# A selective scan on one Trainium2 core: in each step ScalarE does the preparation's work before the unit's decay instead of after it

## The chip, the core and the metric

The kernel runs on one core of a Trainium2 chip. The core has five engines that matter here, each with an instruction queue of its own that is worked off in order: TensorE (PE, matmuls into PSUM), VectorE (DVE), ScalarE (ACT), GpSimd (POOL) and SyncE (SP, which issues most DMAs). They meet only at semaphores. The metric is device microseconds from start to end of one execution. All times below are of single executions or medians of them.

## What is computed

The input is x, 8 images of 96 channels and 64x64 pixels. A first layer (a 17x17 depthwise convolution, a pointwise product, gelu, a gate) gives a new x of the same shape. The second layer takes each image as a sequence of 4096 tokens and runs a selective scan over it, forward and backward:

```
xn = layernorm(x) * ln_g + ln_b
x, z = split(xn @ W_in)
x = silu(causal_conv(x, conv_w, conv_b))
proj = x @ W_xproj
dt = softplus(proj[:6] @ W_dt + b_dt)
Bm, Cm = proj[6:22], proj[22:38]
h = exp(dt * A) * h + dt * Bm * x        # along the tokens, 192 channels x 16 states
y = sum over states(h * Cm) + x * D
out = forward((y * silu(z)) @ W_out) + the same backward
```

The change lies in the scan, which is most of the time.

## The kernel before, in words

The scan works on pieces of 1024 tokens (T), 4 pieces of each of 8 images, each piece forward and backward: 64 *rounds* (`LAST = 2 * ITERS`), a loop of 32 iterations with two directions in each. The 192 channels x 16 states of a piece are 3072 rows, cut into 24 *units* (`UNITS`) of 128 rows. For a unit n:

- ScalarE makes the decay exp(dt*A), 128x1024 (L1116), into one of 4 `decay` tiles, or for the five units in `POOL_UNITS = (2, 6, 11, 15, 19)` into a PSUM tile `u_ps`. Right behind it it copies the last column of the scan of unit n-4 to `ends` (L1132), which raises `kept`. Both wait for a scan: the decay of unit n for the scan of n-4 (of n-3 for a unit of the five), the copy for the scan of n-4.
- TensorE spreads B over the rows into one of three `u_ps` tiles (L1029), after the scan of n-3; VectorE multiplies it by dt*x (`drive`, L1204). For the five units GpSimd makes that product instead (`drive_p`, L1246), and TensorE and VectorE have nothing to do for them there.
- VectorE scans along the tokens (L1222) into one of four `hring` tiles. It waits for the decay, the product, the `kept` of unit n-4 and the `c_applied` of unit n-4, that is until GpSimd has read the `hring` tile that is to be written again.
- GpSimd multiplies the scan by C (`hc`, L1259) and raises `c_applied`. TensorE sums over the states into `y_ps` (L1047, two units at a time), ScalarE copies that to `y_sb` every eighth unit (L1180), SyncE stores it.

Beside this runs the *preparation* of the next rounds, a share of it in each of the 24 steps. All its products go through one PSUM bank, `prep_ps`. TensorE writes it, ScalarE copies it out and raises `prep_out`, TensorE writes the next product:

- step 0: ScalarE takes silu of the convolved x (`xa`, L1149), between two loads of its function table;
- step 2: TensorE makes the low-rank product (L1081, L1084), step 3: ScalarE copies it to `low` (L1155);
- steps 4, 6, 8: TensorE makes three parts of dt (L1091, L1091, L1095). Steps 5, 7, 9: ScalarE takes |dt| to `soft` (L1165) and relu to `dt_sb` (L1166); at 7 (parts one and two together) and at 9 it takes exp and then ln of `soft` (L1169, L1171), which raises `soft_step`;
- steps 7 and 9: GpSimd adds `soft` and `dt_sb` (L1266), which is softplus; steps 8 and 10: it multiplies by `xa` (L1270). Step 5: it splits B (L1273, L1275);
- steps 10 to 20: TensorE does the causal convolution of the round after next in three parts, ScalarE copies them to `xc` (L1139) at steps 13, 17 and 21.

The order on each engine is written out by the helper `run`, the same for all: in step m it calls the tasks in the order in which they are named. "front" does the work on the unit that is 8 ahead (`LEAD = 8`): step m makes the decay of unit m+8. "back" does the output of unit m, "prep" and "conv" the preparation. On GpSimd "front" in step m is the `drive_p` of unit m+10, if there is one, and the `hc` of unit m+5; on VectorE it is the drive of unit m+7 and then the scan of unit m+6. Below, "scan 12" is the scan of unit 12 of the round looked at, "step 7" is step 7 of `run`.

Of the kernel before, what the change touches and what calls it, by code (L numbers as in the profile page):

```python
# [96 lines left out]
def load_exp_ln(nc):  # L97

    nc.scalar.add_instruction(mybir.InstLoadActFuncSet(name=nc.get_next_instruction_name(), act_func_set_id=EXP_LN, ins=[], outs=[]))
# [571 lines left out]
def scan(nc, d, w):  # L671

    with ExitStack() as ctx:
# [149 lines left out]
        def run(eng, *tasks):  # L823

            def ahead(kind, pn):
                for m in range(UNITS):
                    for has, what in tasks:
                        if has == kind:
                            what(m, pn, 0, pn)

            ahead("conv", 0)
            ahead("prep", 0)
            for n in range(LEAD):
                for kind, what in tasks:
                    if kind == "front":
                        what(n, n, 0, 0)
            ahead("conv", 1)
            with eng.Fori(0, ITERS) as it:
                for dr in range(2):
                    p = 2 * it + dr  # L840
                    for m in range(UNITS):
                        n = m + LEAD
                        where = (n, it, dr) if n < UNITS else (n - UNITS, it + dr, 1 - dr)
                        for kind, what in tasks:
                            if kind == "front":
                                what(UNITS * p + n, *where)
                            elif kind == "back":
                                what(m, p, it, dr)
                            elif kind == "prep":
                                what(m, p + 1, it + dr, 1 - dr)  # L850
                            else:
                                what(m, p + 2, it + 1, dr)
                    for kind, what in tasks:
                        if kind == "back":
                            what(UNITS, p, it, dr)

        with nc.Block() as block:
# [156 lines left out]
            def _(pe):  # L1014
# [17 lines left out]
                def back(m, p, it, dr):  # L1032

                    if m == UNITS:
                        return
                    g = m // 8
                    if m % 2:
                        n0 = m - 1
                        pe.wait_ge(c_applied, UNITS * p + n0 + 2)
                        if n0 % 8 == 0:  # L1040

                            pe.wait_ge(y_ready, NG * p + g)
                        for n in (n0, n0 + 1):
                            _, q, b = group(n)
                            for i in range(2):
                                at = 32 * (2 * b + i)
                                last = nc.tensor.matmul(y_ps[at:at + 32, :], w["gather"][:, :], hc[n % NHC][:, i * SL:(i + 1) * SL],  # L1047
                                                        start=(q == 0), stop=(q == QN - 1))
                        last.then_inc(summed, 2)
                    if m % 8 == SKIP_AT:  # L1050
                        for b in range(2):
                            for i in range(2):
                                at = 32 * (2 * b + i)
                                if g < 2:
                                    rows, cols, steps = slice(0, P), slice(64 * g + 32 * b, 64 * g + 32 * b + 32), PART[i]
                                else:
                                    rows, cols, steps = slice(64 * i, 64 * i + 64), slice(P + 32 * b, P + 32 * b + 32), PART[2]
                                nc.tensor.matmul(y_ps[at:at + 32, :], w["skip"][rows, cols], xa[dr][rows, steps], start=False, stop=False)
# [42 lines left out]
            def _(act):  # L1101
# [79 lines left out]

                act.wait_ge(zeroed, 1)
                load_exp_ln(nc)
                run(act, ("back", back), ("front", front), ("prep", prep), ("conv", conv))

            @block.vector
            def _(dve):
# [312 lines left out]
```

## Time and profile before

| | us |
|---|---|
| time, median of 3 runs (lowest to highest) | 6072.25 (6064.57 to 6073.67) |
| the profiled execution's own time | 6072.92 |
| its span, first to last instruction | 6071.1 |
| VectorE busy | 5288.1 |
| GpSimd busy | 5088.1 |
| TensorE busy, matmuls | 4711.1 |
| ScalarE busy | 3204.5 |

The span has three stages: the first layer and the normalisation until about 880 us, the scan until about 5800 us, the output projection from there to the end. Busy time is the union of the instructions' times on an engine; the shares are of the whole span. An idle time of an engine is put down to what released it, inferred from semaphores: where an instruction waits for several, it is the one that came last by the profile.

### The profile page before, as it was taken

Reading aid. Unit: us, or ns where it says so; the run is one execution under the profiler, and the core shown is the slowest. Engines: PE = TensorE matmul, PEld = TensorE weight load, DVE = VectorE, ACT = ScalarE, POOL = GpSimd, SP = SyncE. Lnnn points to the kernel's source line nnn. Section 1 sums busy time; section 2 is a strip of 40 time slices with the busy share of each in tenths; the row PEclk is TensorE's granted clock in tenths of the full one; section 3 lists DMA queues with packets and bytes.
Section 4 is the critical chain, followed back from the end, with each engine's and each line's share of the span. In section 5 each row is a group of like instructions: output and inputs, shape, how many; then the busy total and the mean of one; then the engine's idle time right before and its main releaser. Section 6 shows DMA issues by size and latency. Waiting matters only on the chain. (4 is left out here: it accounts for less than half of the span.)

```text
span 6071.1 us, 73617 instructions
## 1 busy us (share of the span) xinstructions
PE 4711.1 (78%) x17230; PEld 1200.4 (20%) x17230; DVE 5288.1 (87%) x3523; ACT 3204.5 (53%) x5159; POOL 5088.1 (84%) x2405
## 2 busy tenths in 40 slices
PE   7998757777777777777777777777777777777788
PEld 6775211111111111111111111111111111111122
DVE  3223749999999999999999999999999999999943
ACT  1224645555555555555555555555555555555533
POOL 0000349999999999999999999999999999999965
PEclk9999876666676666666666666666666666666689
DMA  1002755555555555555555555555555555555599
GB/s 35 28 28 67 213 152 183 184 183 183 184 184 184 184 184 182 182 181 181 182 181 181 182 183 184 184 184 183 182 182 184 184 184 182 183 183 182 182 260 274
DMA packets 351020, 1048.25 MB, mean 173 GB/s; under 512 B 66820, under 2 KB 101430, under 8 KB 300556
## 3 DMA queue, kind: packets, MB, share of 16 engines
q1 hardware_dynamic: 336652, 1022.72, 53.2%
q10 hardware_dynamic: 14336, 25.17, 1.3%
q8 instruction: 12, 0.20, 0.0%
q14 instruction: 20, 0.16, 0.0%
HBM read 836.01 MB, written 211.63 MB: 173 GB/s over the span
## 5 line engine op out<-in xcount | busy, mean ns | idle before, releaser
L1259 POOL TENSOR_TENSOR hc<-hring,c_rep 128x1024 f32<-128x1024 f32 x1541 | 3597.5, 2361 | 18.9 <-DVE hring L1222 13.6
L1222 DVE TENSOR_TENSOR_SCAN hring<-decay,carry,u_ps 128x1024 f32<-128x1024 f32 x1221 | 2827.7, 2333 | 44.3 <-POOL hc L1259 44.3
L1029 PE MATMUL u_ps<-stack_b,w_spread 48*128 48x512 bf16 x2442 | 1053.8, 523 | 908.0 <-DVE hring L1222 904.0
L1116 ACT ACTIVATE decay<-dt_rep,w_a 128x1024 f32<-128x1024 f32 x1222 | 1399.5, 1147 | 675.2 <-DVE hring L1222 662.4
L1204 DVE TENSOR_TENSOR u_ps<-u_ps,u_rep 128x1024 f32<-128x1024 f32 x1221 | 1471.5, 1205 | 68.3 <-DMA u_rep<-u_scr 56.4
L1047 PE MATMUL y_ps<-hc,w_gather 128*32 128x512 f32 x6144 | 1212.4, 874 | 0.0
L1116 ACT ACTIVATE u_ps<-dt_rep,w_a 128x1024 f32<-128x1024 f32 x322 | 360.0, 1118 | 1360.7 <-DVE hring L1222 1360.7
L1246 POOL TENSOR_TENSOR drive_p<-u_rep,b_rep 128x1024 f32<-128x1024 f32 x322 | 760.2, 2361 | 11.1 <-DMA u_rep<-u_scr 11.1
L1222 DVE TENSOR_TENSOR_SCAN hring<-u_ps,carry,drive_p 128x1024 f32<-128x1024 f32 x321 | 751.3, 2341 | 11.6 <-ACT decay L1116 11.6
L666 POOL TENSOR_TENSOR xs<-xc_ln,rs 96x512 f32<-96x512 f32 x64 | 90.3, 1411 | 701.9 <-ACT rs L650 684.2
L1029 PEld LDWEIGHTS u_ps<-stack_b,w_spread 48*128 48x128 bf16 x2442 | 147.4, 101 | 2407.3 <-DVE hring L1222 2004.4
L1068 PE MATMUL prep_ps<-xn,w_conv 128*128 128x512 f32 x792 | 587.6, 848 | 45.4 <-DMA xn<-xn_scr 23.6
L294 PE MATMUL pc<-xpad,toep 128*128 128x256 f32 x1728 | 468.3, 401 | 2.6 <-DVE toep L191 0.6
L191 DVE COPY toep<-pw 128x288 f32<-128x288 f32 x200 | 91.5, 457 | 326.6 <-PE pw L273 326.6
L294 PEld LDWEIGHTS pc<-xpad,toep 128*128 128x128 f32 x1728 | 296.0, 190 | 37.8 <-issue 11.3
L1266 POOL TENSOR_TENSOR dt_sb<-soft,dt_sb 128x1024 f32<-128x1024 f32 (+1 forms) x130 | 237.0, 1823 | 77.3 <-ACT soft L1171 77.3
L1095 PE MATMUL prep_ps<-low,w_dt 6*64 6x512 f32 x260 | 128.1, 1083 | 186.8 <-ACT dt_sb L1166 186.8
L1132 ACT COPY ends<-hring 128x1 f32<-128x1 f32 x1540 | 270.7, 176 | 0.0
L1071 PE MATMUL prep_ps<-xn,w_conv 128*64 128x512 f32 x792 | 254.2, 727 | 1.6 <-ACT xc L1139 1.6
L191 ACT COPY toep<-pw 128x288 f32<-128x288 f32 x200 | 79.9, 399 | 330.1 <-PE pw L273 330.1
L1047 PEld LDWEIGHTS y_ps<-hc,w_gather 128*32 128x32 f32 x6144 | 140.2, 126 | 554.8 <-issue 410.1
L1091 PE MATMUL prep_ps<-low,w_dt 6*128 6x512 f32 x260 | 203.6, 873 | 59.2 <-ACT low L1155 57.8
(108 smaller groups left out, 3966.9 us busy)
## 6 DMA issues: line engine op xcount, KB each, us to landing
dt_rep<-dt_scr SPq DMA_DIRECT2D x194, 1024.0 KB, 5.8
u_rep<-u_scr SPq DMA_DIRECT2D x194, 1024.0 KB, 7.7
c_rep<-bc_scr SPq DMA_DIRECT2D x260, 512.0 KB, 4.0
b_rep<-bc_scr SPq DMA_DIRECT2D x130, 512.0 KB, 4.2
xn<-xn_scr SPq DMA_DIRECT2D x132, 384.0 KB, 5.4
y_scr<-y_sb SPq DMA_DIRECT2D x768, 64.0 KB, 1.6
xn<-xn_scr SPq DMA_DIRECT2D x132, 256.0 KB, 4.7
dt_scr<-dt_sb SPq DMA_DIRECT2D x260, 128.0 KB, 2.1
```

The lines of the kernel that those rows point to most:

```text
L294: last = nc.tensor.matmul(pc[c][:, 0:B * XH].rearrange("p (b x) -> p b x", b=B), toep[par][:, n0:n0 + 2, :].rearrange("p a y -> p (a y)"), ...
L1029: mm = nc.tensor.matmul(u_ps[nv % NSLOT][:, sl], w["spread"][:, q, :], upper(stack_b[drv][:, sl]), start=True, stop=True)
L1047: last = nc.tensor.matmul(y_ps[at:at + 32, :], w["gather"][:, :], hc[n % NHC][:, i * SL:(i + 1) * SL], start=(q == 0), stop=(q == QN - 1))
L1068: mm = nc.tensor.matmul(prep_ps[:, :], w["conv"][:, j, 0:P], xn[:, j, PART[g]], start=(j == 0), stop=(j == 2))
L1071: mm = nc.tensor.matmul(prep_ps[64 * s:64 * s + 64, :], w["conv"][:, j, P:DI], xn[:, j, PART[s]], start=(j == 0), stop=(j == 2))
L1116: nc.scalar.activation(to[:, :], dt_rep[r][:, b, :], ACT.Exp, scale=w["a"][:, col:col + 1]).then_inc(decay_ready, 1)
L1132: nc.scalar.copy(ends[:, drv, nv:nv + 1], hring[nv % NHR][:, end:end + 1]).then_inc(kept, 1)
L1204: nc.vector.tensor_tensor(slot[:, :], slot[:, :], u_rep[r][:, b, :], ALU.mult).then_inc(drive_ready, 1)
L1222: nc.vector.tensor_tensor_scan(hring[nv % NHR][:, ::step], factor[:, ::step], term[:, ::step], carry[:, drv, nv:nv + 1], ALU.mult, ALU.add ...
L1246: nc.gpsimd.tensor_tensor(drive_p[k % 2][:, :], u_rep[r][:, b, :], b_rep[q][:, :], ALU.mult).then_inc(pool_drive, 1)
L1259: nc.gpsimd.tensor_tensor(hc[nv % NHC][:, :], hring[nv % NHR][:, :], c_rep[q][:, :], ALU.mult).then_inc(c_applied, 1)
L1266: nc.gpsimd.tensor_tensor(dt_sb[:, HALVES[h]], soft[:, HALVES[h]], dt_sb[:, HALVES[h]], ALU.add).then_inc(dt_ready, 1)
```

## The change

One line: the order of the tasks in ScalarE's steps.

```diff
-                run(act, ("back", back), ("front", front), ("prep", prep), ("conv", conv))
+                run(act, ("back", back), ("prep", prep), ("conv", conv), ("front", front))
```

The order of instructions on the other four engines is the same as before. On ScalarE two places are shown. The first is step 7 of the first direction, which makes the part of `soft` that GpSimd adds first: `u_ps0` is the decay of unit 15. Before:

```order
L1116 ACTIVATE decay2<-dt_rep1,w_a 128x1024
L1132 COPY ends<-hring2 128x1
L64 REGISTER_ALU
L1116 ACTIVATE u_ps0<-dt_rep1,w_a 128x1024
L1131 REGISTER_ALU
L1132 COPY ends<-hring3 128x1
L1164 REGISTER_ALU
L1165 ACTIVATE soft<-prep_ps,w_dt_b 128x512
L1166 ACTIVATE dt_sb<-prep_ps,w_dt_b 128x512
L1169 ACTIVATE soft<-soft 128x1024
L1170 ISA
L1171 ACTIVATE soft<-soft 128x1024
```

And now:

```order
L1116 ACTIVATE decay2<-dt_rep1,w_a 128x1024
L1132 COPY ends<-hring2 128x1
L1164 REGISTER_ALU
L1165 ACTIVATE soft<-prep_ps,w_dt_b 128x512
L1166 ACTIVATE dt_sb<-prep_ps,w_dt_b 128x512
L1169 ACTIVATE soft<-soft 128x1024
L1170 ISA
L1171 ACTIVATE soft<-soft 128x1024
L64 REGISTER_ALU
L1116 ACTIVATE u_ps0<-dt_rep1,w_a 128x1024
L1131 REGISTER_ALU
L1132 COPY ends<-hring3 128x1
```

The five instructions of the preparation moved ahead of the decay of unit 15 and of the copy behind it.

The second is step 0 of the second direction, on ScalarE: the silu and its two table loads stand behind the decay of unit 8 before, and ahead of it now. Piece of the order before, from the copy of `y_ps` that ends the round:

```order
L1180 COPY y_sb<-y_ps 128x512
L64 ISA
L1113 ISA
L1116 ACTIVATE decay<-dt_rep,w_a 128x1024
L1132 COPY ends<-hring 128x1
L64 REGISTER_ALU
L1149 ACT_TABLE_LOAD
L1149 ACTIVATE xa<-xc 128x1536
L99 ACT_TABLE_LOAD
```

And now:

```order
L1180 COPY y_sb<-y_ps 128x512
L64 REGISTER_ALU
L1149 ACT_TABLE_LOAD
L1149 ACTIVATE xa<-xc 128x1536
L99 ACT_TABLE_LOAD
L64 ISA
L1113 ISA
L1116 ACTIVATE decay<-dt_rep,w_a 128x1024
L1132 COPY ends<-hring 128x1
```

What moved is the block of silu, up to the end of the round before; the decay of unit 8 and all decays behind it stand behind that block. In the other steps with preparation work (3, 5, 9, 13, 17, 21) it moved up in the same way by one decay and one copy of a column.

## Rows read from the trace of the kernel before

**Rows 1.** The page's part 1: busy us, share of the span, instructions.
```profile
PE 4711.1 (78%) x17230; PEld 1200.4 (20%) x17230; DVE 5288.1 (87%) x3523; ACT 3204.5 (53%) x5159; POOL 5088.1 (84%) x2405
```
**Rows 2.** Groups by line, whole span: busy us, mean ns | idle before, releaser.
```profile
L1259 POOL TENSOR_TENSOR hc<-hring,c_rep 128x1024 f32<-128x1024 f32 x1541 | 3597.5, 2361 | 18.9 <-DVE hring L1222 13.6 <-issue 3.2
L1222 DVE TENSOR_TENSOR_SCAN hring<-decay,carry,u_ps 128x1024 f32<-128x1024 f32 x1221 | 2827.7, 2333 | 44.3 <-POOL hc L1259 44.3
L1222 DVE TENSOR_TENSOR_SCAN hring<-u_ps,carry,drive_p 128x1024 f32<-128x1024 f32 x321 | 751.3, 2341 | 11.6 <-ACT decay L1116 11.6
L1266 POOL TENSOR_TENSOR dt_sb<-soft,dt_sb 128x1024 f32<-128x1024 f32 (+1 forms) x130 | 237.0, 1823 | 77.3 <-ACT soft L1171 77.3
```
**Rows 3.** Line 1122, once a round: ns min/median/max, first and last start us.
```profile
L1122 ACT COPY carry<-ends x64: 193/194/198, 915.9 to 5726.4; 128x24 f32 x64
```
**Rows 4.** Timeline, VectorE: start us, us, line, operation, count [idle before <-releaser].
```profile
2982.07 2.33 DVE L1222 TENSOR_TENSOR_SCAN hring<-decay,carry,u_ps 128x1024 f32<-128x1024 f32 x1
...
2993.31 1.20 DVE L1204 TENSOR_TENSOR u_ps<-u_ps,u_rep 128x1024 f32<-128x1024 f32 x1
...
2998.92 1.20 DVE L1204 TENSOR_TENSOR u_ps<-u_ps,u_rep 128x1024 f32<-128x1024 f32 x1
...
3002.29 1.20 DVE L1204 TENSOR_TENSOR u_ps<-u_ps,u_rep 128x1024 f32<-128x1024 f32 x1
...
3006.77 2.33 DVE L1222 TENSOR_TENSOR_SCAN hring<-decay,carry,u_ps 128x1024 f32<-128x1024 f32 x1
3009.82 2.35 DVE L1222 TENSOR_TENSOR_SCAN hring<-decay,carry,u_ps 128x1024 f32<-128x1024 f32 x1 [0.71 <-POOL hc L1259]
...
3013.47 2.35 DVE L1222 TENSOR_TENSOR_SCAN hring<-u_ps,carry,drive_p 128x1024 f32<-128x1024 f32 x1 [0.18 <-ACT decay L1116]
...
3016.92 2.35 DVE L1222 TENSOR_TENSOR_SCAN hring<-decay,carry,u_ps 128x1024 f32<-128x1024 f32 x1
```
**Rows 5.** Timeline, GpSimd, the same round.
```profile
2984.49 2.37 POOL L1259 TENSOR_TENSOR hc<-hring,c_rep 128x1024 f32<-128x1024 f32 x1
...
2998.07 2.37 POOL L1266 TENSOR_TENSOR dt_sb<-soft,dt_sb 128x1024 f32<-128x1024 f32 x1 [1.14 <-ACT soft L1171]
...
3007.37 2.36 POOL L1259 TENSOR_TENSOR hc<-hring,c_rep 128x1024 f32<-128x1024 f32 x1
...
3010.91 2.38 POOL L1259 TENSOR_TENSOR hc<-hring,c_rep 128x1024 f32<-128x1024 f32 x1
...
3014.47 2.36 POOL L1259 TENSOR_TENSOR hc<-hring,c_rep 128x1024 f32<-128x1024 f32 x1
```
**Rows 6.** Timeline, ScalarE, steps 6 and 7 of that round.
```profile
2987.77 0.18 ACT L1132 COPY ends<-hring 128x1 f32<-128x1 f32 x1
2993.42 1.12 ACT L1116 ACTIVATE u_ps<-dt_rep,w_a 128x1024 f32<-128x1024 f32 x1 [5.47 <-DVE hring L1222]
...
2994.56 0.68 ACT L1165 ACTIVATE soft<-prep_ps,w_dt_b 128x512 f32<-128x512 f32 x1
...
2996.94 1.06 ACT L1171 ACTIVATE soft<-soft 128x1024 f32<-128x1024 f32 x1
```
**Rows 7.** Timeline, TensorE's matmuls, steps 6, 8 and 9 of that round.
```profile
2987.25 1.39 PE L1091 MATMUL prep_ps<-low,w_dt 6*128 6x512 f32 x2
...
2995.87 1.97 PE L1095 MATMUL prep_ps<-low,w_dt 6*64 6x512 f32 x4 [2.90 <-ACT dt_sb L1166]
2997.77 1.03 PE L1029 MATMUL u_ps<-stack_b,w_spread 48*128 48x512 bf16 x2
```
**Rows 8.** Timeline, the round's end and step 0 of the next, ScalarE and VectorE.
```profile
3044.02 0.57 ACT L1180 COPY y_sb<-y_ps 128x512 f32<-128x512 f32 x1
...
3046.47 1.28 ACT L1149 ACT_TABLE_LOAD   x1
...
3050.56 1.15 ACT L1116 ACTIVATE decay<-dt_rep,w_a 128x1024 f32<-128x1024 f32 x1
...
3055.11 2.33 DVE L1222 TENSOR_TENSOR_SCAN hring<-decay,carry,u_ps 128x1024 f32<-128x1024 f32 x1
```

## The prediction

> **What bounds the kernel now.** Start with the groups by line. In the scan VectorE and GpSimd are nearly always busy, and the idle time in front of their instructions is short and regular [rows 2]: VectorE waits 44.3 us for `hc` and 11.6 us for something put down to ScalarE, GpSimd waits 77.3 us for `soft` in front of L1266. GpSimd waits for VectorE only 13.6 us in the whole scan. The carry copy comes once a round, so a round takes (5726.4 - 915.9) / 63 = 76.36 us [rows 3].
>
> Now one round in the timelines. On VectorE a product and a scan repeat every 3002.29 - 2998.92 = 3.37 us, and where GpSimd made the product of the next unit the distance is 2998.92 - 2993.31 = 5.61 us for two units [rows 4]. A round has 19 products on VectorE, 5 of them followed by such a double: 14 x 3.37 + 5 x 5.61 = 75.23 us. So the round is 1.13 us longer than VectorE's work.
>
> Where it loses that: scan 17 starts at 3006.77, and scan 18, a double, would start 5.61 - 3.37 = 2.24 later; it starts 3.05 later, a loss of 0.8. From there to scan 19 it is 3.65 instead of 3.37, a loss of 0.28, and to scan 20 3.45, a loss of 0.08 [rows 4]. Together 1.16, the 1.13 within reading. Each of the three scans may begin once GpSimd has read the `hring` tile of four units ago. `hc` 14 ends at 3007.37 + 2.36 = 3009.73, scan 18 starts at 3009.82. `hc` 15 ends at 3013.29, scan 19 starts at 3013.47. `hc` 16 ends at 3016.83, scan 20 starts at 3016.92 [rows 4, 5]. The wait of scan 19 is named after ScalarE's decay, but the decay of unit 19 was made two scans earlier, so I read it as GpSimd's too.
>
> GpSimd is late there because of one pause. `hc` 9 starts at 2984.49 [rows 5], 0.09 us after scan 9 ended (2982.07 + 2.33 = 2984.40) [rows 4]: there GpSimd has caught up with VectorE. Then it works without a gap until step 7, and waits 1.14 us there for the `soft` of ScalarE [rows 5]; 77.3 us for 65 of them are 1.19 each [rows 2]. GpSimd's own round is therefore 76.36 - 1.14 = 75.22 us.
>
> And ScalarE is late by its own order. In step 7 it waits 5.47 us, from 2987.95 (end of the copy of step 6) to 2993.42, for scan 12, since the decay of unit 15 stands first. Only then come |dt|, relu, exp and ln, 2994.56 to 2998.00, that is 3.44 us [rows 6]. TensorE's product that they read had been there since 2987.25 + 1.39 = 2988.64 [rows 7].
>
> The chain is: scan 12, decay 15, `soft`, the sum on GpSimd, `hc` 14, scan 18. VectorE pays for it in each of 64 rounds.
>
> **What the change does, part by part.**
>
> *Step 7.* `soft` no longer waits for scan 12. ScalarE is free at 2987.95, the product is there at 2988.64, plus 3.44 makes 2992.1 instead of 2998.0: 5.9 us earlier. GpSimd wants it at 2998.07 - 1.14 = 2996.93, so the pause goes with 4.8 us to spare. Its cover would be gone only if TensorE's product came that much later; the products of steps 2 to 6 are made no later than now, since `low` and the first part of dt are copied earlier as well.
>
> *What is late next.* With the pause gone, all of GpSimd behind step 7 comes 1.14 us earlier. Scan 18 needs 0.8 of that, scan 19 0.8 + 0.28 = 1.08, scan 20 1.16: all three waits go, the last with nothing over. Then VectorE's 75.23 and GpSimd's 75.22 us are equal, and so is the way through both: GpSimd's stretch from `hc` 9 allows scan 20 at 3016.92 - 1.14 = 3015.78, and VectorE alone would reach it at 3006.77 + 2.24 + 2 x 3.37 = 3015.75 [rows 4, 5]. So the round falls to the work of VectorE and no further. Of the 1.13 us I count 1.10; 0.03 is for the tie.
>
> *The decays behind the preparation.* No work is added: the instructions are the same, and per step with preparation one decay and one copy come later by what stands before them. The largest block is silu at step 0, from 3046.47 to 3050.56 = 4.09 us. It can start when the copy of `y_ps` ends, 3044.59, so decay 8 starts at 3048.7 and ends at 3049.8 instead of 3046.4. Scan 8 starts at 3055.11 [rows 8]: 5.3 us of cover. Costed at 0. The copies of a column behind the decays raise `kept` for the same scans and have the same cover. In step 7 decay 15 waits for scan 12 anyway (2993.42 [rows 6]) and the block before it ends at 2992.1: nothing. In steps 3, 5, 9, 13, 17 and 21 the blocks are one or two copies and at step 9 the exp and ln of one part, all shorter than the silu, before decays that have two or three scans of cover: 0.
>
> Weighed against the Trainium skill: here two table loads of 1.28 us [rows 8] and the silu fill the 4.09 us with no gap. "ScalarE: Activation LUTs", section "What ACT_TABLE_LOAD costs", puts a switch at about 2.66 us, since a drain of about 1.38 us comes on top. By it the block would be some 2.7 us longer, decay 8 still in time, and the sum unchanged; the row shows no such drain here.
>
> *TensorE.* It waits 2.90 us in step 8 for the relu of step 7 [rows 7]. That goes, since the relu comes 5.9 us earlier. Today the spread of unit 16 behind it ends at 2998.80 [rows 7], only 0.12 before VectorE's product of unit 16 at 2998.92 [rows 4]; it gets earlier, so this does not become a wait. If TensorE had no slack elsewhere this would help too, but nothing is credited for it.
>
> *SyncE's queue.* The stores of `low`, `dt_sb` and `y_sb` are issued as soon as their makers are done, so earlier or at the same time; none is moved past another. Costed at 0.
>
> **The sum.** 64 rounds x 1.10 = 70.4 us. The bounds: at least 0.8 a round, if only the wait in front of scan 18 goes (51 us), at most 1.16 (74 us). The first layer and the output projection are not touched. The profiled execution took 6072.92 us, 0.67 above the median of 6072.25, so it stands for the median. 6072.25 - 70.4 = 6001.9.
>
> **The rivals.**
>
> *Only the first wait goes.* For it speaks that the profile names ScalarE's decay in front of scan 19 (11.6 us in all [rows 2]), and that three chains tie at 75.2. Then 0.36 us a round stays and the saving is 0.8 x 64 = 51 us: 6021. Against it: `hc` 15 ended at 3013.29, just ahead of scan 19.
>
> *Nothing changes.* GpSimd's pause is replaced by another one, because what it does next also hangs on the round (a load of `u_rep`, the split of B), or because TensorE's product comes late once ScalarE asks early. Then GpSimd's 1.14 us stays in some place and the time is 6072. Against it: GpSimd waits in steady state for nothing else than `soft` and, four times at the start, VectorE [rows 2]. The Trainium skill would come to the same time by a rule: "Perfetto Trace Analysis", section "Identifying the Most-Contended Engine", says to optimise the engine with the highest occupancy first. ScalarE has 53%, VectorE 87% and GpSimd 84% [rows 1], so an edit of ScalarE's order would be worth nothing. The 1.14 us pause speaks against reading it that way.
>
> *Slower: ScalarE's queue is held by the preparation.* Now a decay stands behind a copy that waits for TensorE. If a product comes so late that the decay passes its cover, VectorE waits. The tightest place is decay 8 with 5.3 us. It decides from a delay of 5.3 us on, and costs more than the gain from 5.3 + 1.13 = 6.4 us. A delay of 7.6 us would cost 2.3 - 1.13 = 1.2 us a round, 77 us: 6149. Against it: the longest pause of TensorE that the rows show is 2.90 us.
>
> **How the numbers follow.** All waits go, 5998 to 6008: 0.68. Only the first: 0.18. Nothing: 0.08. Slower: 0.04. The remaining 0.02 lie between the second and the third. The prediction is 6001.9. The range runs from 5996 (1.16 a round, and 2 us for the spread of runs) to 6036, which takes in the second case with a third of its saving lost; it leaves out the third and the fourth. Within 0.2%, about 12 us and what a measurement can tell from no change, lies nearly only the third case: same 0.08. Faster 0.88, slower 0.04.
>
> **What the profile after would show.** GpSimd's idle time before L1266 falls from 77.3 us to the first one's few us. The idle times of VectorE before L1222 (44.3 and 11.6) fall under 5 together. The carry copies stand 75.25 us apart. GpSimd starts to wait briefly for VectorE at `hc`. ScalarE's silu starts right behind the copy of `y_ps`. TensorE's wait before L1095 is gone. If the second case is right, about 0.3 us stays before scan 19 and the round is 75.6. The forecast is wrong if GpSimd has a new regular pause, or if VectorE waits for a decay that was made late.

## The result and the profile after

The changed kernel takes 5995.43 us, median of 4 runs (5991.95 to 5998.44), against 6071.51 us (6064.57 to 6073.67) for the kernel before in the same comparison: a ratio of 0.9876, 95% interval 0.9859 to 0.9894. It is 76 us faster, 1.2%. The forecast was 6001.9, 70 us less than before, with a range of 5996 to 6036: the gain is as forecast in kind and 6 us larger. The median lies below the low end of the range by 0.6 us, which is less than the spread of the runs (6.5 us).

The profiled execution took 5995.97 us, its span is 5994.1 us. The groups by line of the kernel after, with the same columns as [rows 2]:

```profile
L1259 POOL TENSOR_TENSOR hc<-hring,c_rep 128x1024 f32<-128x1024 f32 x1541 | 3597.8, 2360 | 21.2 <-DVE hring L1222 14.3 <-issue 3.2
L1222 DVE TENSOR_TENSOR_SCAN hring<-decay,carry,u_ps 128x1024 f32<-128x1024 f32 x1221 | 2821.8, 2333 | 0.0
...
L1222 DVE TENSOR_TENSOR_SCAN hring<-u_ps,carry,drive_p 128x1024 f32<-128x1024 f32 x321 | 751.3, 2340 | 0.0
...
L1266 POOL TENSOR_TENSOR dt_sb<-soft,dt_sb 128x1024 f32<-128x1024 f32 (+1 forms) x130 | 236.3, 1818 | 3.2 <-ACT soft L1171 3.2
```

VectorE's 44.3 and 11.6 us of idle time before its scans are gone, to the last tenth. GpSimd's 77.3 us before L1266 are 3.2, a single wait. The mean durations are the same within 5 ns. The carry copy, which is made once a round, as in [rows 3]:

```profile
L1122 ACT COPY carry<-ends x64: 193/195/198, 914.9 to 5651.9; 128x24 f32 x64
```

(5651.9 - 914.9) / 63 = 75.19 us a round instead of 76.36. In the stretch from 912 to 5650 us of the kernel after, busy time of each engine (stretch, length, then PE, PEld, DVE, ACT, POOL):

```profile
912.00:5650.00 4738.00, 3673.80 (x12472) 630.12 (x12468) 4738.00 (x2708) 2742.44 (x4350) 4726.40 (x2204) 0.67 0.57 186
```

VectorE is busy for all 4738.00 us. GpSimd lacks 11.6 us of it: three waits of 1.0 us for VectorE at the start, and 8.6 us in gaps too short to be listed, about 0.14 us a round. The row of the same stage of the kernel before has 98.9% for VectorE and 98.3% for GpSimd:

```profile
912.00:5726.00 4814.00, 3683.84 (x12478) 629.90 (x12478) 4758.98 (x2711) 2737.10 (x4352) 4731.99 (x2205) 0.67 0.56 183
```

Step 7 of one round after, ScalarE (to be held against [rows 6]):

```profile
2955.58 0.17 ACT L1132 COPY ends<-hring 128x1 f32<-128x1 f32 x1
2957.61 0.69 ACT L1165 ACTIVATE soft<-prep_ps,w_dt_b 128x512 f32<-128x512 f32 x1 [1.86 <-PE prep_ps L1091]
...
2959.99 1.06 ACT L1171 ACTIVATE soft<-soft 128x1024 f32<-128x1024 f32 x1
2961.26 1.12 ACT L1116 ACTIVATE u_ps<-dt_rep,w_a 128x1024 f32<-128x1024 f32 x1 [0.21 <-DVE hring L1222]
```

`soft` is ready at 2961.05, before the decay of unit 15, which still starts when scan 12 lets it. GpSimd and VectorE in the same round:

```profile
2964.74 2.37 POOL L1266 TENSOR_TENSOR dt_sb<-soft,dt_sb 128x1024 f32<-128x1024 f32 x1
```
```profile
2958.90 2.33 DVE L1222 TENSOR_TENSOR_SCAN hring<-decay,carry,u_ps 128x1024 f32<-128x1024 f32 x1
```

GpSimd reaches its sum at 2964.74, 3.7 us after `soft`, and does not stop. Scan 12 is the lower row: it ends at 2961.23.

### The profile page after: what moved, and what is told of

The parts are those of the page before. It is cut to its first block and busy times, and to the rows that moved or that the text cites. A ratio compares the mean times of both kernels' runs of the same rounds, so it can differ in the third digit from the quotient of the medians.

```text
span 5994.1 us, 73617 instructions
## 1 busy us (share of the span) xinstructions
PE 4704.2 (78%) x17230; PEld 1201.4 (20%) x17230; DVE 5272.6 (88%) x3523; ACT 3212.3 (54%) x5159; POOL 5086.2 (85%) x2405
## 5 line engine op out<-in xcount | busy, mean ns | idle before, releaser
L1204 DVE TENSOR_TENSOR u_ps<-u_ps,u_rep 128x1024 f32<-128x1024 f32 x1221 | 1473.3, 1207 | 68.2 <-DMA u_rep<-u_scr 55.7
L1132 ACT COPY ends<-hring 128x1 f32<-128x1 f32 x1540 | 271.1, 176 | 0.0
L1139 ACT ACTIVATE xc<-prep_ps,w_conv_b 128x512 f32<-128x512 f32 x198 | 136.0, 687 | 231.7 <-PE prep_ps L1068 181.3
L1338 POOL TENSOR_TENSOR ys<-yf,yb 96x1024 f32<-96x1024 f32 x64 | 161.0, 2516 | 100.5 <-DMA xz<-xn_scr 100.5
L1058 PE MATMUL y_ps<-xa,w_skip 128*32 128x512 f32 (+1 forms) x1536 | 245.9, 719 | 0.0
```

Of the source, the lines that this page charges most:

```text
L1132: nc.scalar.copy(ends[:, drv, nv:nv + 1], hring[nv % NHR][:, end:end + 1]).then_inc(kept, 1)
L1204: nc.vector.tensor_tensor(slot[:, :], slot[:, :], u_rep[r][:, b, :], ALU.mult).then_inc(drive_ready, 1)
```

## The experiments

**Step 7 alone.** Only step 7 of the preparation goes ahead of the decay:

```diff
+                def first(m, pn, it, dr):
+                    if m == 7:
+                        prep(m, pn, it, dr)
+
+                def then(m, pn, it, dr):
+                    if not (m == 7):
+                        prep(m, pn, it, dr)
...
-                run(act, ("back", back), ("prep", prep), ("conv", conv), ("front", front))
+                run(act, ("back", back), ("prep", first), ("front", front), ("prep", then), ("conv", conv))
```

> Only step 7 of the preparation moves ahead of ScalarE's decay; all other steps stand as before the change. If GpSimd's pause for soft in step 7 is the whole cause: 5996, the time after the change, within 6 us, with no idle time of VectorE before its scans. If the earlier copies of the other steps (low, the first part of dt, the convolution) carry a part: in between, 6010 to 6060.

5998.79 us (5993.87 to 6001.96), ratio to before 0.9881 (0.9864 to 0.9897). That is the time of the whole change within what is measured, and its round is (5654.1 - 916.3) / 63 = 75.20 us:

```profile
L1122 ACT COPY carry<-ends x64: 192/194/198, 916.3 to 5654.1; 128x24 f32 x64
```

**All but step 7.** The same split, with `m != 7` in the place of `m == 7`, and the convolution's copies ahead too.

> The mirror image: every step of the preparation moves ahead of the decay but step 7. If step 7 is the whole cause: 6071, as before, with the pause of about 1.14 us before line 1266 in each round and VectorE's three waits. If the other steps carry a part: under 6055.

6071.24 us against 6071.94, ratio 0.9998 (0.9989 to 1.0008): no change, to about 0.1%. The waits are those of before, in the groups by line of this kernel:

```profile
L1230 DVE TENSOR_TENSOR_SCAN hring<-decay,carry,u_ps 128x1024 f32<-128x1024 f32 x1221 | 2829.9, 2335 | 44.5 <-POOL hc L1267 44.5
...
L1230 DVE TENSOR_TENSOR_SCAN hring<-u_ps,carry,drive_p 128x1024 f32<-128x1024 f32 x321 | 752.1, 2343 | 11.6 <-ACT decay L1116 11.6
...
L1274 POOL TENSOR_TENSOR dt_sb<-soft,dt_sb 128x1024 f32<-128x1024 f32 (+1 forms) x130 | 236.9, 1822 | 77.3 <-ACT soft L1171 77.3
```

The two kernels together say it: of the eight steps that the change reorders on ScalarE (0, 3, 5, 7, 9, 13, 17, 21), step 7 is worth 1.2% and the others nothing that can be measured.

**The pause taken away on GpSimd instead.** ScalarE's order is that of before. GpSimd takes its first sum one step later:

```diff
-        SUM_AT = (7, 9)
-        U_AT = (8, 10)
+        SUM_AT = (8, 9)
+        U_AT = (9, 10)
```

> ScalarE's order as before the change; GpSimd takes its first softplus sum in step 8 instead of 7 and the product behind it in step 9 instead of 8, so it reaches the sum 2.3 us later and finds soft ready. Pause theory (what counts is that GpSimd does not stand still): 5996 to 6002. Rival (what counts is something that ScalarE does earlier): 6071.

5997.02 us (5993.62 to 5999.8), ratio 0.9881 (0.9864 to 0.9897). With ScalarE as late as ever, GpSimd just does another `hc` first (three in a row instead of two) and reaches the sum when `soft` is there:

```profile
2960.65 7.00 POOL L1259 TENSOR_TENSOR hc<-hring,c_rep 128x1024 f32<-128x1024 f32 x3
2967.62 2.36 POOL L1266 TENSOR_TENSOR dt_sb<-soft,dt_sb 128x1024 f32<-128x1024 f32 x1
```

VectorE's waits are gone too, the one named after ScalarE's decay among them, though ScalarE's order was not touched:

```profile
L1222 DVE TENSOR_TENSOR_SCAN hring<-u_ps,carry,drive_p 128x1024 f32<-128x1024 f32 x321 | 751.3, 2341 | 0.0
```

So it is GpSimd's pause that cost the time, and not anything that ScalarE does earlier.

**Is GpSimd at its limit too?** The changed kernel, with two 128x128 tiles of zeros added up on GpSimd in step 7, for nobody:

```diff
+                    if m == 7:
+                        nc.gpsimd.tensor_tensor(idle_out[:, 0:P], idle_in[:, 0:P], idle_in[:, 0:P], ALU.add)
```

> The changed kernel, and GpSimd adds two 128x128 pieces of zeros in step 7 of each round, 0.40 to 0.46 us, that nobody needs. If GpSimd and VectorE are tied, the round grows by 0.2 to 0.45 us: 6010 to 6024. If VectorE alone bounds it with room on GpSimd: 5996.

6018.55 us (6014.81 to 6020.6), 23 us more than the changed kernel. A round is (5671.6 - 913.7) / 63 = 75.52 us, 0.33 longer. The instruction itself takes 0.39 us, but the next one starts before it has ended, so that it holds GpSimd up by 2972.80 - 2972.45 = 0.35 us:

```profile
2972.45 0.39 POOL L1267 TENSOR_TENSOR idle_out<-idle_in 128x128 f32<-128x128 f32 x1
2972.80 2.36 POOL L1271 TENSOR_TENSOR dt_sb<-soft,dt_sb 128x1024 f32<-128x1024 f32 x1
```

So after the change GpSimd has at most a few hundredths of a microsecond of room in 75. The wait that comes back tells something besides:

```profile
L1225 DVE TENSOR_TENSOR_SCAN hring<-u_ps,carry,drive_p 128x1024 f32<-128x1024 f32 x321 | 752.0, 2343 | 10.0 <-ACT decay L1118 6.4
```

Only GpSimd's work was made longer, ScalarE's order and work are those of the changed kernel, and yet 6.4 us are put down to ScalarE's decay, at the same form of scan as the 11.6 us of [rows 2]. The name is that of the semaphore that the profile puts last, not that of the cause.

**Is VectorE a bound of its own?** Softplus as ln(1 + exp(dt)), two ScalarE instructions where there were four, and no sum on GpSimd. In exact arithmetic it is the same function.

```diff
-                        nc.scalar.activation(soft[:, PART[g]], prep_ps[:, :], ACT.Abs, bias=w["dt_b"][:, h:h + 1])
-                        nc.scalar.activation(dt_sb[:, PART[g]], prep_ps[:, :], ACT.Relu, bias=w["dt_b"][:, h:h + 1]).then_inc(prep_out, 1)
+                        nc.scalar.activation(soft[:, PART[g]], prep_ps[:, :], ACT.Exp, bias=w["dt_b"][:, h:h + 1]).then_inc(prep_out, 1)
...
-                            nc.scalar.activation(soft[:, HALVES[h]], soft[:, HALVES[h]], ACT.Exp, scale=-1.0).then_inc(soft_step, 1)
-                            act.wait_ge(soft_step, 2 * (2 * pn + h) + 1)
-                            nc.scalar.activation(soft[:, HALVES[h]], soft[:, HALVES[h]], ACT.Ln, bias=1.0).then_inc(soft_step, 1)
+                            nc.scalar.activation(dt_sb[:, HALVES[h]], soft[:, HALVES[h]], ACT.Ln, bias=1.0).then_inc(dt_ready, 1)
...
-                        if m == SUM_AT[h]:
-                            pool.wait_ge(soft_step, 2 * (2 * pn + h) + 2)
-                            nc.gpsimd.tensor_tensor(dt_sb[:, HALVES[h]], soft[:, HALVES[h]], dt_sb[:, HALVES[h]], ALU.add).then_inc(dt_ready, 1)
```

> The changed kernel with softplus taken as ln(1 + exp(dt)) by two ScalarE instructions, so GpSimd's two sums of a round (2.33 + 1.24 us) fall away, and nothing else. VectorE's work stays 75.2 us a round. If VectorE is a bound of its own: 5996, although GpSimd has 3.6 us less to do. If GpSimd is what sets the round: down to 5770.

5993.11 us (5988.17 to 5999.71): the time of the changed kernel, though GpSimd has 3.6 us a round less to do. The round is (5653.1 - 916.3) / 63 = 75.19 us. GpSimd now stands and waits for VectorE:

```profile
L1256 POOL TENSOR_TENSOR hc<-hring,c_rep 128x1024 f32<-128x1024 f32 x1541 | 3601.8, 2359 | 237.7 <-DVE hring L1219 234.5
```

**And what GpSimd gained, given to VectorE's side.** The same kernel with one more unit's product on GpSimd:

```diff
-POOL_UNITS = (2, 6, 11, 15, 19)
+POOL_UNITS = (2, 6, 11, 15, 19, 23)
...
-        B_AT = (11, 7)
+        B_AT = (11, 15)
```

> As the kernel before it, and GpSimd takes the product of a sixth unit (23) from VectorE; the load of the B rows that it reads moves from step 7 to 15. VectorE: 12 x 3.37 + 6 x 5.61 = 74.1 us a round, GpSimd: 75.2 - 3.6 + 2.3 = 73.9. Expected: 1.1 us a round less, 5925. If a third engine (TensorE, whose work no longer pauses) bounds it: 5996.

5921.16 us (5917.79 to 5924.01), ratio to before 0.9754 (0.9738 to 0.9771), 74 us under the changed kernel. A round is (5573.5 - 907.8) / 63 = 74.06 us, as worked out, and this is the fastest kernel of the study:

```profile
L1122 ACT COPY carry<-ends x64: 192/194/198, 907.8 to 5573.5; 128x24 f32 x64
```

**How much cover the late decays have.** The changed kernel, with seven copies of a 128x1024 tile of zeros on ScalarE behind silu in step 0, in front of the decay of unit 8:

```diff
+                        for k in range(7):
+                            wait(act, idled, 7 * pn + k, k > 0 or pn)
+                            nc.scalar.copy(idle_out[:, :], idle_in[:, :]).then_inc(idled, 1)
```

> The changed kernel with seven such copies behind silu in step 0, in front of the decay of unit 8: 7.3 to 8 us. Cover in the trace after: 5.3 us (the decay ends at 2941.29, scan 8 starts at 2946.55). The excess of 2.0 to 2.8 us stays with VectorE in each round: 128 to 180 us more, 6124 to 6176, with one wait of VectorE for ScalarE a round. If a late decay is absorbed: 5996.

6161.37 us (6159.06 to 6165.17), ratio to before 1.0151 (1.0134 to 1.0168). ScalarE and VectorE in one round:

```profile
2935.78 7.51 ACT L1156 COPY idle_out<-idle_in 128x1024 f32<-128x1024 f32 x7
2943.19 1.15 ACT L1119 ACTIVATE decay<-dt_rep,w_a 128x1024 f32<-128x1024 f32 x1
```
```profile
2944.55 2.35 DVE L1229 TENSOR_TENSOR_SCAN hring<-decay,carry,u_ps 128x1024 f32<-128x1024 f32 x1 [2.45 <-ACT ends L1135]
```

The copies delay the decay by 2943.19 - 2935.78 = 7.4 us, and VectorE waits 2.45 us once a round for what stands behind them (the row names the copy of a column that follows the decay, L1135). So 5.0 us were free, against 5.3 read before. A round is (5821.5 - 926.2) / 63 = 77.70 us, 2.51 longer than in the changed kernel and 1.34 longer than before the change. This is the third rival of the prediction brought about on purpose: held back by 7.4 us, the decay makes the kernel slower than before. From which delay on, no run shows; 5.0 us of cover and the 1.17 us gained give about 6.2 us, an estimate, where the prediction had 6.4.

**How much cover `soft` has.** Five such copies in step 7, in front of |dt|.

> The changed kernel with five copies of a 128x1024 tile of zeros on ScalarE in step 7, one after the other and in front of |dt|. Taken at 1.05 to 1.15 us each (the decay of the same size takes 1.15) they make soft 5.2 to 5.8 us later. The cover in the trace after is 3.7 us (soft ends at 2961.05, GpSimd reaches the sum at 2964.74), so the pause comes back with 1.5 to 2.1 us a round. If it costs VectorE its full size: 96 to 134 us more, 6092 to 6130. If GpSimd has room: less.

6001.13 us (5996.33 to 6006.03), 6 us more than the changed kernel and not the 96 to 134 expected. A round is (5658.0 - 918.9) / 63 = 75.22 us, against 75.19. The expectation had a mistake in it:

```profile
2960.35 5.35 ACT L1170 COPY idle_out<-idle_in 128x1024 f32<-128x1024 f32 x5
2965.60 0.68 ACT L1172 ACTIVATE soft<-prep_ps,w_dt_b 128x512 f32<-128x512 f32 x1
```

In the changed kernel ScalarE stands 1.86 us in front of |dt| for TensorE's product. The copies fill that time first, so `soft` comes only 5.25 - 1.86 = 3.4 us later, within the 3.7 us of cover. GpSimd's idle time before the sum is 8.0 us in the whole run, 3.2 in the changed kernel. The run confirms that nearly all of the cover is there; what a pause costs beyond it was not tried.

**Four runs that did not test what they were meant to.** An earlier form of the two dose experiments took repeated loads of ScalarE's function table as filler: three and six of them in step 0, two and four in step 7.

> The changed kernel with three more loads of ScalarE's table (1.28 us each, 3.85 together) behind silu in step 0, in front of the decay of unit 8. In the trace after, that decay ends at 2941.29 and scan 8 starts at 2946.55: 5.3 us of cover. If the cover is as read: no change, 5996. If a decay that stands behind the preparation is already at its limit: up to 3.85 us a round more, up to 6240.

> The same with six more loads, 7.7 us. The cover of 5.3 us is passed by 2.4 to 2.6 us a round: 154 to 166 us more, 6150 to 6162, and VectorE waits for the decay or the column copy of ScalarE once a round. If ScalarE could catch up elsewhere: less.

> The changed kernel with two more table loads on ScalarE in step 7, in front of |dt| (2.57 us). In the trace after, soft ends at 2961.05 and GpSimd reaches the sum at 2964.74: 3.7 us of cover. Expected: no change, 5996.

> The same with four more loads, 5.14 us: GpSimd's pause in front of the sum comes back with 5.14 - 3.7 = 1.4 us a round. If the pause costs VectorE its full size, as GpSimd has no room left: 90 us more, 6086. If part of it is absorbed: 6010 to 6060.

They took 5993.99, 5994.8, 5997.85 and 5997.16 us, all the time of the changed kernel. The traces tell why, first that of the run with six more loads in step 0, then that of the run with four more in step 7:

```profile
L99 ACT ACT_TABLE_LOAD x67 | 86.0, 1283 | 8.0 <-DVE ends L1194 6.9
```
```profile
L99 ACT ACT_TABLE_LOAD x132 | 169.4, 1283 | 9.3 <-DVE ends L1195 7.0
```

In step 0 the loads were to stand right behind the load that is there anyway. The trace has 67 loads at that line, as without them: none was added, for three as for six. In step 7, with other instructions before them, 132 - 67 = 65 were added, one a round, for two as for four. In both places a row of equal loads, one right behind another, came down to one. The single load of 1.28 us in step 7 fell into the time in which ScalarE waits for TensorE anyway:

```profile
2954.45 1.28 ACT L99 ACT_TABLE_LOAD   x1
2956.30 0.69 ACT L1168 ACTIVATE soft<-prep_ps,w_dt_b 128x512 f32<-128x512 f32 x1 [0.56 <-PE prep_ps L1091]
```

The wait in front of |dt| is 0.56 us in place of 1.86, and `soft` comes no later. The first and the third of the four would have looked like confirmations of "no change".

## Why the prediction was right, point by point

**What bounds the round.** Right. VectorE's work was read as 75.23 us a round, and the round is now 75.19. GpSimd's own round was read as 75.22, a tie with VectorE's; 0.35 us more for GpSimd made the round 0.33 longer, so the tie is there within a few hundredths.

**The three waits of VectorE have one cause.** Right, the third named "ACT decay" included. It stayed at 11.6 us when all of ScalarE's steps but step 7 were moved, went to 0.0 when only GpSimd's sum was moved, and came back when only GpSimd was given more to do. The first rival, that only the first wait goes (6021), is out.

**Step 7.** Right in kind. The cover of `soft` was put at 4.8 us and is 3.7 in the rows shown. Against the end of scan 12, GpSimd reaches the sum 3.5 us later in both kernels. But TensorE's product for |dt| is ready 4.7 us before that end in the round that the prediction read, and 3.7 us before it in the round read after the change (2961.23 - 2957.57). Scan 12 and the product before, and the product after:

```profile
2991.05 2.33 DVE L1222 TENSOR_TENSOR_SCAN hring<-decay,carry,u_ps 128x1024 f32<-128x1024 f32 x1
```
```profile
2987.25 1.39 PE L1091 MATMUL prep_ps<-low,w_dt 6*128 6x512 f32 x2
```
```profile
2955.50 2.07 PE L1091 MATMUL prep_ps<-low,w_dt 6*128 6x512 f32 x2
```

This is not something that the change did. The same product takes 1.34 to 2.07 us from round to round in both kernels, with a median of 2.07 in both: here one of 2.07 before the change and one of 1.41 after it.

```profile
4057.04 2.07 PE L1091 MATMUL prep_ps<-low,w_dt 6*128 6x512 f32 x2
```
```profile
2052.29 1.41 PE L1091 MATMUL prep_ps<-low,w_dt 6*128 6x512 f32 x2
```

What differs in the rows is TensorE's granted clock. It was 0.99 of full speed, the level of 2.4 GHz, from 2987 to 2988 us before the change, and 0.50, the level of 1.2 GHz, from 2955.5 to 2957.6 us after it. It had stood at 1.00 from 2948 to 2954 us, with a wait of 1.68 us for scans within it, and then fell (stretch, length, busy time of PE, PEld, DVE, ACT, POOL, granted clock):

```profile
2987.00:2988.00 1.00, 1.00 (x4) 0.29 (x2) 1.00 (x2) 0.95 (x2) 1.00 (x1) 0.99 0.00 0
```
```profile
2955.50:2957.60 2.10, 2.07 (x3) 0.49 (x2) 2.10 (x2) 0.25 (x2) 2.10 (x2) 0.50 0.00 0
```

So the prediction took its cover from a round with a quick product. Over the 63 rounds after the change the time from the end of `soft` to GpSimd's sum is 3.1 to 4.8 us, 3.7 in the median: even the least of it is enough. The sentence that TensorE's products come no later than now was too strong; it cost nothing here. ScalarE does wait for them now, which it hardly did before (2.7, 27.6 and 4.3 us in the three groups below), as the waits of ScalarE from 912 to 5650 us show (who waited <- for whom: us, times, longest):

```profile
ACT low L1155 <- PE prep_ps L1084: 199.4, 62, 3.4
ACT xc L1139 <- PE prep_ps L1068: 153.3, 109, 3.2
ACT soft L1165 <- PE prep_ps L1091: 120.2, 77, 2.4
```

In exchange ScalarE's decays wait less for scans. It is idle time of an engine that is not the bottleneck, and with a round of 75.19 us, VectorE's own work, it costs nothing. TensorE's wait before L1095 is gone as forecast, 1.4 us in all instead of 186.8.

**The decays behind the preparation.** Right, costed at 0 with 5.3 us of cover at the tightest place; the run with seven copies put the cover at 5.0. The block of silu with its two table loads takes 4.09 us after the change (2940.14 - 2936.05) as before, with no drain to be seen. The figure of the Trainium skill that was weighed ("ScalarE: Activation LUTs", section "What ACT_TABLE_LOAD costs"), a drain of about 1.38 us on top of the load in each switch, is not borne out by this case.

```profile
2936.05 1.28 ACT L1149 ACT_TABLE_LOAD   x1
...
2940.14 1.15 ACT L1116 ACTIVATE decay<-dt_rep,w_a 128x1024 f32<-128x1024 f32 x1
```

**The sum.** 64 x 1.10 = 70.4 us was forecast. The term for a round was too small. Measured, a round became 76.36 - 75.19 = 1.17 us shorter, 64 x 1.17 = 74.9 us. That is 0.07 us a round more: the 0.03 kept back for the tie was not needed, and VectorE's work is 0.04 less than the sum of rounded distances. The remaining 2 us of the span lie behind the scan, in the output projection (from the issue of its first weights to the end 6071.1 - 5800.0 = 271.1 us before and 5994.1 - 5725.0 = 269.1 after). Nothing was changed there, and one execution of each does not tell a cause.

**The rule on the most-contended engine** (the Trainium skill, "Perfetto Trace Analysis", section "Identifying the Most-Contended Engine"). The prediction read it as saying that an edit on the 53% engine is worth nothing, 6072, and that is out as a forecast. The page says less: it names the engine to optimise for first, not where the edit has to be made. What it asks for agrees with this case, since the gain is VectorE's idle time; only the place to change was two engines away. The 77.3 us that GpSimd waited for ScalarE became 56 us of waiting on VectorE in the profile, and 75 us in its distances.

## What to carry to other kernels

Where two engines are both over 98% busy in the steady stretch, as here, look for the regular pause of the one that the other waits for, and follow it to the engine that is hardly busy: the order of work in that queue may be what costs. Put work that a bottleneck waits for ahead of work that has whole steps of slack, and count that slack in the trace. Once both engines are full and even, moving a wait brings nothing more; only less work does, and then both engines must get less, as the two kernels with the shorter softplus show.

## What had not been expected

- With GpSimd less busy, in the kernel with the shorter softplus and five units, VectorE's instructions look longer while the pace stays: the product took 1240 ns in the median instead of 1207 in the changed kernel, and a round still 75.19 us. Why they look longer, no run shows. Where instructions of an engine overlap, as these do, the distances of their starts tell the pace and their durations do not.
- VectorE lost more than its idle rows say. They add to 44.3 + 11.6 = 56 us, the distances between starts to 1.17 x 64 = 75. The rest is overlap that a late start loses (about 0.1 us each at scans 18 and 19), and a delay that is not listed at all, the 0.08 us before scan 20.
